# Sums of exponentials one unit later, and another order of SyncE's first transfers, in a two-layer attention kernel

## The reference

```
xn  = group_norm(x) * gamma + beta                  # 32 groups
q, k, v = split(w_qkv @ xn + b_qkv)                 # 8 heads x 32 channels, 1024 pixels
m   = softmax((q * scale)^T (k * scale))            # 1024 x 1024 for each head
a   = m applied to v
x   = x + w_proj @ a + b_proj
```

## Time and profile before

| | |
|---|---|
| Median of three runs | 2264.74 us |
| The profiled execution's own time | 2263.78 us |
| Its span | 2262.0 us |
| PE busy | 2193.9 us (97%) |
| DVE, ACT, POOL busy | 1692.7, 1274.0, 1788.2 us (75, 56, 79%) |
| Chain that ended last, by engine | PE 89%, DVE 4%, issue 3% |
| PE's granted clock, mean | 0.986 of full speed |

### The profile page before, as it was taken

How to read it: one execution, slowest core, us unless ns; L and a number is a source line. 1 busy time by engine, 2 the same in 40 slices (tenths; PEclk the granted TensorE clock), 3 DMA queues, 4 the chain that set the end, 5 groups by cost and what they waited for, 6 DMA issues and landing times.

```text
span 2262.0 us, 41861 instructions
## 1 busy us (share of the span) xinstructions
PE 2193.9 (97%) x10552; PEld 1091.3 (48%) x10552; DVE 1692.7 (75%) x2896; ACT 1274.0 (56%) x2321; POOL 1788.2 (79%) x567
## 2 busy tenths in 40 slices
PE   5799999999999999999999999999999999999998
PEld 3355454545545455454544545445454544545442
DVE  3677787777877778777777878768777777877772
ACT  2355656566565555656555565655656556565554
POOL 2388878888887978878887888878878788788785
PEclk8799999999999999999999999999999999999999
DMA  4222233322333322233322333222333322433210
GB/s 118 57 69 49 53 95 76 95 43 56 72 75 96 68 68 53 57 95 94 89 40 63 81 76 94 62 61 55 71 94 76 79 45 51 93 76 76 52 43 20
DMA packets 208771, 157.53 MB, mean 70 GB/s; under 512 B 166528, under 2 KB 166784, under 8 KB 208512
## 3 DMA queue, kind: packets, MB, share of 16 engines
q1 hardware_dynamic: 208512, 154.48, 29.8%
HBM read 36.39 MB, written 16.78 MB: 24 GB/s over the span
## 4 chain that ended last, share of the span: by engine, by line
PE 89%; DVE 4%; issue 3%; SPq 1%; ACT 1%; DMA 1%; DVEq 1%; POOL 0%; ACTq 0%; POOLq 0%
PE ps_t L365 25%; PE ps_v L400 21%; PE ps_m L382 19%; PE ps_d L421 9%; PE ps_a L413 5%; PE ps_d L436 5%; PE ps_d L429 5%; SPq L254 1%; DVE raw_max L656 1%; DVE stage_ql L673 1%; DVE att L717 1%; ACT pt L582 1%; DVE rden L707 0%; DMA qs<-neg_max 0%; PE ps_m L421 0%
## 5 line engine op out<-in xcount | busy, mean ns | idle before, releaser
L656 DVE TENSOR_REDUCE raw_max<-ps_m 128x1 f32<-128x512 f32 x2048 | 1332.4, 684 | 444.1 <-PE ps_m L382 413.4
L582 ACT ACTIVATE pt<-ps_t 128x512 f32<-128x512 f32 x2048 | 1141.8, 596 | 919.3 <-PE ps_t L365 913.0
L828 POOL TENSOR_TENSOR acc<-acc,pt 128x2048 f32<-128x2048 f32 x317 | 1448.8, 4570 | 89.5 <-ACT pt L582 61.5
L382 PE MATMUL ps_m<-ks,qs 96*128 96x512 f32 x2048 | 988.0, 483 | 9.0 <-DVE raw_max L656 8.0
L365 PE MATMUL ps_t<-qs,ks 97*128 97x512 f32 x2048 | 879.0, 430 | 30.3 <-issue 13.1
L365 PEld LDWEIGHTS ps_t<-qs,ks 97*128 97x128 f32 x2048 | 389.6, 191 | 656.4 <-ACT pt L582 366.9
L828 POOL TENSOR_TENSOR acc<-pt 128x2048 f32<-128x2048 f32 x64 | 291.8, 4560 | 327.0 <-ACT pt L582 327.0
L400 PE MATMUL ps_v<-pt,v 128*32 128x512 f32 x4096 | 546.5, 606 | 0.0
L382 PEld LDWEIGHTS ps_m<-ks,qs 96*128 96x128 f32 x2048 | 393.0, 192 | 152.2 <-issue 62.7
L421 PE MATMUL ps_d<-xn,wq 128*128 128x512 f32 x500 | 262.7, 608 | 8.2 <-ACT xn L614 5.7
L400 PEld LDWEIGHTS ps_v<-pt,v 128*32 128x32 f32 x4096 | 80.7, 108 | 185.1 <-ACT pt L582 115.1
(11 more groups left out here) (46 smaller groups left out, 531.9 us busy)
## 6 DMA issues: line engine op xcount, KB each, us to landing
ks<-stage_kh SPq DMA_DIRECT2D x256, 128.0 KB, 2.5
qs<-stage_qh SPq DMA_DIRECT2D x256, 128.0 KB, 2.5
ks<-stage_kl SPq DMA_DIRECT2D x128, 128.0 KB, 2.5
qs<-stage_ql SPq DMA_DIRECT2D x128, 128.0 KB, 2.5
qs<-neg_max SPq DMA_DIRECT2D x1024, 0.5 KB, 2.0
xn<-x_dram SPq DMA_DIRECT2D x16, 512.0 KB, 4.0
res<-x_dram SPq DMA_DIRECT2D x16, 512.0 KB, 4.2
between<-res SPq DMA_DIRECT2D x32, 256.0 KB, 2.1
```

Of the source, the lines that this page charges most:

```text
L382: pe.matmul(ps_m[max_bank(u)][:, :], qs[b][0:KROWS, h, c:c + P], ks[b][0:KROWS, h, kf * HALF:(kf + 1) * HALF], start=True, stop=True).then ...
L582: act.activation(pt[t % 4][:, h, :], ps_t[u % 2][:, :], ACT.Exp, scale=SCALE).then_inc(exp_done, 1)
L656: dve.tensor_reduce(raw_max[:, e % 2, t, kf:kf + 1], ps_m[max_bank(u)][:, :], AX.X, ALU.max)\
L828: pool.tensor_tensor(acc[hf][:, :, :], a[:, :, :], pt[t % 4][:, :, :], ALU.add).then_inc(pool_added, 1)
```

## The change

`SUMS_AT` goes from 10 to 11. The sums move from behind unit 10 to behind unit 11 (and from 42 to 43), ahead of the weighted values that stand there, and the four division steps on DVE move one unit on with them. At the start SyncE sends the row of head 3 ahead of the staging of slot 1, and stages slot 1's heads one at a time in the slot routine that the other slots use, a row of maxima between them.

```diff
-SUMS_AT = 10
+SUMS_AT = 11
...
             for h in range(HG):
                 stage_head(0, 0, h)
-            for e in range(HG - 1):
+            for e in range(HG):
                 load_row(e, 0, e)
-            for h in range(HG):
-                stage_head(1, 1, h)
-            load_row(HG - 1, 0, HG - 1)
-            for u in range(ROWS_AT, UNITS, MAX_GROUP):
-                slot_row(plain(0), u)
 
             def slot(s, next_layer=None, dsrc=None, ddst=None, done_layer=None, has_next=True):
-                if has_next:
+                if has_next and not (isinstance(s.n, int) and s.n == 0):
 
                     sp.wait_ge(st_ready, UNITS * s.n)
...
-                    if s.g == 0 and piece < CT * NH:
+                    if s.g == 0 and ddst is not None and piece < CT * NH:
                         store_piece(ddst, s.j - 1, s.j - 1 - B * done_layer, piece)
...
+            slot(plain(0))
             turn = B // 2 - 1
```

## The result

The changed kernel takes 2267.49 us, the median of 22 runs (2264.86 to 2272.31), against 2264.7 us (2260.85 to 2269.59, 22 runs) before. The ratio is 1.0014, with a 95% interval of 1.0008 to 1.002: slower by about 3 us. The interval leaves out 1, but the 3 us are less than the 0.2% that I had set as the bound of "same". The forecast was 2273.

A forecast was written before the change was run, and what follows sets the result against it. PE, 97% busy, was taken as the bound, with DVE's list already on its path in 30 second halves. Terms -13.4 - 18.3 + 20.4 + 15.9 + 3.8 = +8.4 us on 2263.8 gave 2272.2, predicted as 2273; range 2250 to 2287.

The forecast's parts named there:

- The start: Before unit 3, PE's 12.45 us wait for a row of maxima shrinks: 13.4 us gained, between 12 and 18.
- The sums on PE: From unit 42's second matmul to unit 44's first, reordering saves 0.29 us at 63 sums: 18.3 us, bounds 0 and 25.
- rival D: Groups of sums and weighted values side by side still cost what they cost apart: 2291 us; chance 0.06.
- DVE's list, second halves: Later division steps delay `qk_low` for unit 49's piece: PE loses 0.68 us at 30 places, 20.4 us.
- The output projection: First halves of g = 0 slots: unit 17 waits for `att`, PE loses 1.06 us at 15 places, 15.9 us.
- The v projection: First halves of g = 1 slots, 15 places: DVE's lag costs PE 0.25 us each, 3.8 us, bounds 0 and 10.
- rival B: Behind seven loop turns PE's low clock loses 1.7 us each; sparing all of it gives 2261 us; chance 0.10.
- Rival A: At units 17 and 49 DVE is done when PE arrives, so only gains stay: 2232 to 2252 us; chance 0.22.
- Rival C: The gain at the start does not come, because what is late next is equally late: 2286 us; chance 0.07.

## Why the prediction was right or wrong

The range was right: 2267.5 lies in 2250 to 2287. The direction was right too, slower having had the most chance, but by 3 us out of terms of 12 to 20 us of either sign; that is less than the low clock moved, so the sign is in part luck. The size was too high by 5.5 us, and by its own bound the outcome was "same", to which I had given 0.21.

- **The start**: 13.4 us foreseen, 12.0 of it from the row and 1.4 from the clock, which was granted at 0.50 from 71.90 on, through the stall and for 8.31 us behind it. The 1.4 us was an estimate of mine that no run shows as such: half of the 2.78 us for which PE was busy in the stretch up to unit 3 (at 0.50 full-width matmuls start 0.43 us apart, 87.69 to 88.12; at the full clock 0.24, 1006.27 to 1006.51). What the runs showed in its place: the row gave 12.4, the clock 0.5 and 1.7 in the two profiles of the changed kernel and 1.7 with SyncE's part alone. The kernels with only this part are 13 to 15 us faster. Right for the row; that the clock's part comes from the missing stall is not shown, since it varies by 1.9 us between kernels that both have the stall.
- **The sums on PE**: 0.29 us foreseen, 0.31 measured at the 60 places of the table; taken for all 63 it is 19.5 in place of 18.3 us. Right, and with it rival D falls: groups with other operands side by side start 0.86 us apart.
- **DVE's list, second halves**: 6.22 us foreseen from unit 44's first matmul to the one behind the piece, 6.15 measured; 0.61 in place of 0.68 us at 30 places, 18.3 in place of 20.4.
- **The output projection**: 1.06 us foreseen, 0.97 measured, 14.6 in place of 15.9 at 15 places.
- **The v projection**: 0.25 chosen between 0 and 0.68, 0.29 measured. That it came so near is luck: no row had shown it.
- **The sum** of these terms as measured, the clock left out, is -12.4 - 19.5 + 18.3 + 14.6 + 4.4 = +5.4 us. The working has +9.8 for the same terms, and +8.4 with its 1.4 us of clock. So the mechanism held, and 4.4 us of the forecast's excess are small errors of these five terms, of which the largest is DVE's list in the second halves, 2.1 us.
- **The low clock** is the term that was mis-sized most. Beyond the start the forecast put it at nothing and kept it as rival B. In the two profiles it gives the changed kernel 0.5 us at the start, 1.4 for one point of the loop fewer, and 2.9 for the long stretch near the end, 4.8 in all. From the fourth row to the end of the span the changed profile is 0.2 us shorter than the one before (2191.2 against 2191.4); the terms with the clock give +0.6. The sums alone bear this out: 17.8 - 0.8 - 2.8 - 2.9 gives +11.3, and the time went up by 11.6.
- **Over all runs** the clock goes the same way. Its mean is 0.985 in the 24 runs of the kernel before that ran beside the experiments, and 0.990 in the 33 runs of the changed kernel. With the levels 0.5 and 1.0 of the profiles that is some 21 us less at the low level, 12.4 of which are the stall at the start; half of the rest, an estimate of 4 us, was gained. From +5.4 that leads near the +2.8 of the medians.
- **Rival A** (DVE's lag hidden) is refuted by the 30 and 14 waits. **Rival B** (the clock) held in part: not seven points but six have the idle time, five of them low before and four or three after, at 1.4 us and not 1.7, and the stretch near the end, which it did not name, is worth more. **Rival C** is refuted by SyncE's order alone.

What I had not seen: that the loss is no price of PE's new order. It is that of the four division steps that the constant `SUMS_AT` drags along, and these can stay where they were. With them held back, the same PE list gives 2227 us.

## What to carry to other kernels

When one constant places work on two engines, ask for each engine by itself whether it should move: here PE wanted the sums later and DVE wanted its steps where they were. Look, too, at an engine that is far from fully busy for the stretch that it works through without a gap: here DVE, busy 74% of the span, stood idle for 2.23 us and then had no gap up to `qk_low`, and a transpose of 0.7 us moved across that line cost PE 0.61 us at each of 30 places. And when two parts of a change go in together, time each alone: here a gain of some 14 us hid a loss of 12.

## What the runs showed of the hardware that I had not expected

Behind an idle time of PE of about 2 us its clock was low for 3.4 us at two to six of six like points of the loop, in ten profiles, at about 1.4 us each; the same kernel had four in one profile and three in another. In kernels that differ by 0.2% this is as large as the effect itself: runs of the kernel before spread from 2260.6 us at a mean clock of 0.987 to 2271.0 at 0.983.
